# A fused convolution, attention and expert kernel: info and mask spread by DMA, not by products with ones

## The reference

```python
x = x + conv(group_norm(x))          # below
t = tokens(x)                        # 32*1024 tokens of 64 channels
t = t + attention(layer_norm(t))     # linear attention with elu+1, 8 heads, a layer norm inside, a 128-wide MLP, a layer norm
t = t + experts(layer_norm(t))       # top 2 of 8 experts, each 64 -> 128 (gelu) -> 64, summed with their weights
...
def conv(x):
    info = relu(info_w @ x + info_b)         # 16 channels
    mask = sigmoid(mask_w @ x + mask_b)      # 16 channels
    expanded = mask[:, None] * info[None]    # all 16*16 = 256 products per pixel
    return relu(out_w @ expanded + out_b)    # back to 64 channels
```

## Time and profile before

| what | us |
|---|---|
| median of 2 runs | 1132.91 (1130.81 to 1135.02) |
| profiled execution | 1131.8 |
| its span, first to last instruction | 1129.9 |
| PE, DVE, ACT, POOL busy | 1038.0, 735.4, 641.0, 404.9 |
| mean granted TensorE clock | 0.985 of full |

### The profile page before, as it was taken

One profiled execution on the slowest core, in us unless ns is written; L12 is line 12 of the kernel. 1 busy time (PEld: TensorE's weight loads), 2 busy tenths in 40 slices (PEclk: granted clock), 3 DMA queues, 4 the chain that ended last, 5 costly groups with the idle time before them and its releaser, 6 DMA issues. The chain is left out here.

```text
span 1129.9 us, 17149 instructions
## 1 busy us (share of the span) xinstructions
PE 1038.0 (92%) x6678; PEld 445.2 (39%) x6678; DVE 735.4 (65%) x1529; ACT 641.0 (57%) x867; POOL 404.9 (36%) x534
## 2 busy tenths in 40 slices
PE   4888699989999899989999899998999989998997
PEld 2453353324533245323543245332454334532232
DVE  5764744786648866587655966488655886646334
ACT  3354356665665655665656556655566655565554
POOL 0010031352323532344323533235333344224576
PEclk9997889999999999999999999999999999999999
DMA  5000095017700464006710078002760057200860
GB/s 162 6 1 1 1 204 136 21 31 166 164 1 20 97 157 106 1 20 149 160 51 1 19 154 205 1 20 54 157 148 1 19 107 167 50 1 19 198 142 19
DMA packets 15600, 88.66 MB, mean 78 GB/s; under 512 B 3488, under 2 KB 6816, under 8 KB 11424
## 3 DMA queue, kind: packets, MB, share of 16 engines
q1 hardware_dynamic: 15520, 87.57, 33.3%
HBM read 78.12 MB, written 9.44 MB: 77 GB/s over the span
## 5 line engine op out<-in xcount | busy, mean ns | idle before, releaser
L1048 POOL TENSOR_TENSOR XB<-TM,XB 128x256 f32<-128x256 f32 x508 | 366.1, 748 | 570.3 <-DVE TM L1360 570.1
L995 ACT ACTIVATE H<-HP,W 128x1024 f32<-128x1024 f32 x224 | 241.4, 1113 | 182.0 <-PE HP L849 181.7
L1360 DVE SCALAR_TENSOR_TENSOR TM<-HP,B2S,CWB 128x512 f32<-128x512 f32 x224 | 164.9, 747 | 163.7 <-PE HP L863 159.2
L849 PE MATMUL HP<-XF,W1E 64*128 64x512 f32 x1024 | 260.8, 620 | 4.4 <-DVE TM L1360 3.7
L863 PE MATMUL HP<-H,W 128*64 128x512 f32 x896 | 234.3, 613 | 24.2 <-ACT H L995 24.2
L849 PEld LDWEIGHTS HP<-XF,W1E 64*128 64x128 f32 x1024 | 86.2, 186 | 129.5 <-issue 59.7
L863 PEld LDWEIGHTS HP<-H,W 128*64 128x64 f32 x896 | 47.7, 135 | 164.9 <-ACT H L995 111.1
L933 ACT ACTIVATE T<-R 128x512 f32<-128x512 f32 x96 | 57.3, 598 | 45.4 <-PE R L642 38.4
L1161 DVE SCALAR_TENSOR_TENSOR BIG<-R,T 128x512 f32<-128x512 f32 x112 | 70.1, 683 | 14.0 <-PE R L606 13.9
L1248 DVE SCALAR_TENSOR_TENSOR BIG<-T,R 128x512 f32<-128x512 f32 x64 | 41.9, 685 | 38.0 <-ACT T L961 38.0
L606 PE MATMUL R<-IM,REP 32*128 32x512 f32 x336 | 51.3, 470 | 7.7 <-DVE RT L1348 4.4
(11 more groups left out here) (182 smaller groups left out, 1398.8 us busy)
## 6 DMA issues: line engine op xcount, KB each, us to landing
CWB<-gates_hbm SPq DMA_DIRECT2D x32, 1536.0 KB, 20.3
CWB<-gates_hbm SPq DMA_DIRECT2D x32, 512.0 KB, 6.6
out<-XB SPq DMA_DIRECT2D x15, 512.0 KB, 3.1
X<-x SPq DMA_DIRECT2D x14, 512.0 KB, 13.5
XF<-x SPq DMA_DIRECT2D x2, 512.0 KB, 5.9
gates_hbm<-RT SPq DMA_DIRECT2D x16, 64.0 KB, 1.6
W<-wpack SPq DMA_DIRECT2D x1, 968.0 KB, 4.7
W1E<-w1e SPq DMA_DIRECT2D x1, 512.0 KB, 7.2
```

The costliest lines, as they stand in the source:

```text
L849: last = mm(HP[u % BATCH][:, half(k)], W1E[img(k), e, :], XF[img(k), 1 - par, s, half(c)], start=True, stop=True)
L995: f(activated(b, u).rearrange("p k t -> p (k t)"), HP[u % BATCH][:, :], ACT.Gelu, bias=col(B1E + e))\
L1048: last = nc.gpsimd.tensor_tensor(acc, TM[:, u % BATCH, quarter(0, h)], acc, ALU.add)
L1360: v.scalar_tensor_tensor(out=TM[:, u % BATCH, :], in0=sums_of(b, u), scalar=B2S[:, e % 2, e // 2:e // 2 + 1], in1=CWB[:, s, e, half(c)], o ...
```

## The change

REP, IM, the 48 matmuls with ones, the 8 ACT copies and the DVE split are taken out. In their place SP issues DMAs as soon as ACT has written a slot's info and mask (im_act). For each slot: two writes of info to HBM (32 partitions, 64 KB each); four mask transfers for image 0, each from 8 partitions of T1 to 128 partitions of BIG, every row copied 16 times (256 KB each, pieces of 2 KB); one info load from HBM to all 128 partitions (512 KB, 16 rows copied 8 times); four mask transfers and one info load for image 1, which goes to XN. DVE then multiplies in place in BIG, 8 products of 1024 columns per group, all operands in SBUF. conv_out waits for all four products of its slot. SP's `prepare` DMAs now stand behind group 0's spreading. SCHEDULE and OPENING are dealt out anew.

```diff
@@ SP (gate_weights, last_weights, store unchanged) @@
+                def replicate(s):
+                    sp.wait_ge(im_act, nth(a + 1, s))
+                    for c in range(NCH):
+                        sp.dma_start(info_hbm[s][:, half(c)], T1a[strip(0, s, c), s, 0:CH]).then_inc(info_out[s], 16)
+                    masks(s, 0)
+                    sp.wait_ge(info_out[s], (a + 1) * 16 * NCH)
+                    info(s, 0)
+                    masks(s, 1)
+                    info(s, 1)
+                def info(s, k):
+                    sp.dma_start(INFO[k][:, s, :], info_hbm[s, IC * k:IC * k + IC, :].unsqueeze(0).broadcast_to([P // IC, IC, T]))\
+                        .then_inc(info_in[k][s], 16)
+                def masks(s, k):
+                    if k == 0 and s == G - 1 and a > EARLY:
+                        sp.wait_ge(lgt_ps, a)
+                    for h in range(2):
+                        for c in range(NCH):
+                            row = strip(1, s, c).start + IC * k + HD * h
+                            sp.dma_start(BIGa[:, s, 2 * k + h, half(c)],
+                                         T1a[row:row + HD, s, 0:CH].unsqueeze(1).broadcast_to([HD, P // HD, CH]))\
+                                .then_inc(mask_in[k][h][s], 16)
+                INFO = (T2a, XNa)
@@ PE @@
-                def replicate(n, slots):
...
-                        for part in range(2):
-                            for c in range(NCH):
-                                rows = strip(1 if n % 3 else 0, s, c)
-                                last = mm(Ra[s][:, half(c)], REP[rows, n, :], IM[rows, s, part, :], start=(part == 0), stop=(part == 1))
                 def conv_out(slots):
...
+                    if exists(a - 1) and a != EARLY:
+                        pe.wait_ge(cwt_done, a)
                     for s, c in pieces(slots):
-                        pe.wait_ge(prod_done[s], at(a * 4 + 4, c))
+                        pe.wait_ge(prod_done[s], a * 4 + 4)
@@ ACT @@
-                def info(k, slots):
-                    for s, c in pieces(slots):
-                        act.wait_ge(rep_ps[s], at(a * NREP + 3 * k + 1, c))
-                        f(T2a[:, s, half(c)], Ra[s][:, half(c)], ACT.Copy).then_inc(ir_done[s], 1)
@@ DVE @@
-                def info_mask(s):
-                    v.tensor_copy(high, T1a[:, s, 0:CH]).then_inc(hl_high, 1)
-                    v.tensor_tensor(IM[:, s, 1, :], T1a[:, s, 0:CH], high.bitcast(F32), ALU.subtract).then_inc(hl_done, 1)
                 def product(k, h, slots):
-                    for s, c in pieces(slots):
-                        if h == 0:
-                            dve.wait_ge(ir_done[s], at(a * 2 + k + 1, c))
-                        dve.wait_ge(rep_ps[s], at(a * NREP + 3 * k + h + 2, c))
-                        v.scalar_tensor_tensor(out=BIGa[:, s, 2 * k + h, half(c)], in0=Ra[s][:, half(c)], scalar=1.0,
-                                               in1=T2a[:, s, half(c)], op0=ALU.add, op1=ALU.mult)\
+                    for s in slots:
+                        dve.wait_ge(info_in[k][s], (a + 1) * 16)
+                        dve.wait_ge(mask_in[k][h][s], (a + 1) * 16 * NCH)
+                        v.scalar_tensor_tensor(out=BIGa[:, s, 2 * k + h, :], in0=BIGa[:, s, 2 * k + h, :], scalar=1.0,
+                                               in1=(T2a, XNa)[k][:, s, :], op0=ALU.add, op1=ALU.mult)\
                             .then_inc(prod_done[s], 1)
@@ SCHEDULE, one of its lines @@
-    ("info_0.1", "YY", 1, 2), ("low_0.0", "", 0, 0), ("low_0.1", "HH", 0, 0), ("high_0.0", "", 0, 0),
+    ("choose_2", "Y", 0, 2), ("info_mask_1", "HYHYHH", 0, 0), ("gate_rows", "Y", 2, 6), ("low_0.1", "YH", 3, 0),
```

More of the change, by code:

```diff
@@ L89 @@
 OPENING = [
[11 rows of a table removed]
-    "norm_4.0", "next conv_out.0", "next centre_1.1", "next centre_1.0", "gates", "next rstd_1", "gate_tokens",
-    "gate_exp", "choose_1", "choose_2", "gate_rows", "weights_1", "next norm_1.1", "next norm_1.0",
-    "next features_1.0", "next features_1.1",
+    "channel_stats", "group_stats", "group_norm", "next channel_stats", "info_mask_0", "info_mask_1", "low_0.0",
[9 rows of a table added]
+    "next centre_1.0", "next centre_1.1", "next rstd_1", "gates", "gate_tokens", "gate_exp", "choose_1", "choose_2",
+    "gate_rows", "next norm_1.0", "next norm_1.1", "next features_1.0", "weights_1", "next features_1.1",
 ]
@@ L254, in build @@
         im_act = sem("im_act")
-        hl_high = sem("hl_high")
-        hl_done = sem("hl_done")
-        rep_ps = sems("rep_ps")
-        ir_done = sems("ir_done")
+        info_out = sems("info_out")
+        info_in = [sems(f"info_in{k}_") for k in range(2)]
+        mask_in = [[sems(f"mask_in{k}{h}_") for h in range(2)] for k in range(2)]
         prod_done = sems("prod_done")
@@ L455, in _ @@
             sp.dma_start(W[:, 0:NW_FIRST], wpack[:, 0:NW_FIRST]).then_inc(w_in, 16)
-            def by_image(t):
-                return t.rearrange("p (k n c) -> p k n c", k=2, c=P)
-            rep = by_image(reps[:, 0:NREP * P])
             im_bias = wpack[:, COLS["cols"][0] + B_IM:COLS["cols"][0] + B_IM + 2]
-            for q in range(4):
-                there = slice(32 * q, 32 * q + 32)
-                sp.dma_start(by_image(raw_reps)[there, :, 0, :], rep[0:32, :, 0, :]).then_inc(r_in, 16)
-                sp.dma_start(by_image(raw_reps)[there, :, 1:3, :], rep[32:64, :, 1:3, :]).then_inc(r_in, 16)
             for q in range(4):
@@ L588, in info_mask @@
                     last.then_inc(im_ps, 1)
-                def replicate(n, slots):
-                    if n == 0 and starting(a):
-                        pe.wait_ge(act_prep, 2)
-                    for s in slots:
-                        if n == 0:
-                            pe.wait_ge(hl_done, nth(a + 1, s))
-                            if exists(a - 1) and a != EARLY:
-                                pe.wait_ge(cwt_done, a)
-                        elif n % 3 == 1:
-                            pe.wait_ge(ir_done[s], at(a * 2 + n // 3 + 1, LAST))
-                        else:
-                            pe.wait_ge(prod_done[s], at(a * 4 + (n + 1) // 3 + n // 3, LAST))
-                        for part in range(2):
-                            for c in range(NCH):
-                                rows = strip(1 if n % 3 else 0, s, c)
-                                last = mm(Ra[s][:, half(c)], REP[rows, n, :], IM[rows, s, part, :], start=(part == 0), stop=(part == 1))
-                                if part == 1:
-                                    last.then_inc(rep_ps[s], 1)
                 def conv_out(slots):
@@ L898, in _ @@
             act.wait_ge(w_in, 16)
[L899 to L900 removed]
             act.wait_ge(bi_in, 128)
             f(BT[:, :], BI[:, 1, 0:1], ACT.Copy, scale=0.5).then_inc(act_prep, 1)
[L903 removed]
+            act.wait_ge(act_prep, 1)
             f(ONE[:, 0:1], BI[:, 0, 0:1], ACT.Copy, bias=1.0, scale=0.0)
@@ L1003, in parts @@
                     "info_mask_0": lambda: info_mask(0), "info_mask_1": lambda: info_mask(1),
-                    **slotwise("info_0", lambda slots: info(0, slots)), **slotwise("info_1", lambda slots: info(1, slots)),
                     **slotwise("conv_out", conv_out), **slotwise("centre_1", lambda slots: square(1, slots)),
```

35 lines of the change are left out of this document (12 added, 23 removed), and 50 rows, old and new, of tables (OPENING, SCHEDULE).

## The result

The changed kernel takes **1566.96 us** (1564.34 to 1569.59, 2 runs), against 1132.91 before: ratio 1.383, 95% interval 1.378 to 1.388. It is slower by 38%. The forecast was 1670 in a range of 1150 to 1800. The profiled execution took 1564.34 us, its span is 1562.5 us, the mean granted clock 0.873.

What follows compares the result with a forecast made beforehand. PE, busy 92% of the span, was taken as the bound before, with DMA setting the interval up to conv_out afterwards. 1131.8 + 408 (six turns) + 131 (opening) = 1671, so 1670 us, range 1150 to 1800.

Steps and rivals of the forecast that it cites:

- Price of a mask transfer: Each 256 KB mask transfer from 8 partitions takes 5.2 us (50 GB/s), between 0.7 and 6.2 us.
- the rate follows the number of partitions touched: DMA rate goes by partitions touched on the SBUF side, not bytes: 381 GB/s for 128, 197 for 64.
- A group in 97 us: A group's DMA work, 16 x 5.2 + 4 x 2.7 + 1.2 = 95 us, lands its last piece at about 97 us.
- A turn +68 us: Each of six turns gets 68 us longer: conv_out at 100 us behind im_act in place of 30.6, 69.4 - 5 + 3.5.
- my -5 for work done early: In each turn, one first and four second expert layers more are done within the interval before conv_out: 5 us less.
- +3.5 for the clock: In each turn PE stands still some 60 us, so afterwards runs partly at 1.2 GHz: 10 x 0.35 = 3.5 us.
- The opening +131 us: The opening, without expert work to fill waits, gets 88 + 46 - 3 = 131 us longer.
- What hides: Router's weights queued behind the masks stay hidden, by a few microseconds; expert units keep their durations; PE slices show six deep gaps.
- Half speed: Rival: a mask transfer takes 2.6 us, a turn is 24 longer, the opening 48: 1324 us (1250 to 1450); chance 0.18.
- Like the router's weights: Rival: a mask transfer takes 1.3 us, a turn +2.5, the opening +23: 1170 us (1145 to 1195); chance 0.15.
- Full speed: Rival: masks at 381 GB/s, 0.7 us each, a group's 18 us hidden under expert layers: 1093 us (1075 to 1115); chance 0.21.
- PE's saving of 7.5 us counts in full: 6 x -7.5: In the full-speed rival, removing 48 matmuls with ones and their waits shortens each of six turns by 7.5 us.

Runs made afterwards that it cites:

- e1_step4: Changed kernel, with each mask transfer's 8 source rows on every 4th partition in place of 8 neighbours; 1285.49 us, ratio 1.134.
- e5_roles: Changed kernel with roles exchanged: mask spread once per image (16 rows on every 2nd partition, 8 copies), info loaded twice per image from HBM; 1188.25 us, ratio 1.050.
- e2_rows128: Changed kernel, but each mask transfer reads all 128 partitions of T1 once (mask wrong, sizes and counts kept); 1195.65 us, ratio 1.055.
- e6_all_fast: Changed kernel, but masks and infos both read all 128 partitions of T1 once, nothing through HBM (mask and info wrong); 1165.17 us, ratio 1.031.
- e7_rows16: Changed kernel, but each mask transfer reads 16 neighbouring rows 8 times in place of 8 rows 16 times (mask wrong); 1312.78 us, ratio 1.160.
- e12_all_fast_old: e6_all_fast with SCHEDULE and OPENING of the kernel before (mask and info wrong); 1148.24 us, ratio 1.013.

## Why the prediction was right

The direction and the chain of waits held, and the sizes were 17 to 26% too large. The rule by which the price was chosen was wrong in its form, and that the price itself came out right is in part luck.

- **Price of a mask transfer**, taken as 5.2 us between 0.7 and 6.2. Transfers by themselves move 50 GB/s, which is 5.2 us. I had it from "the rate follows the number of partitions touched". e1_step4 refutes this as it stands: also 8 partitions, and 136 GB/s; e5_roles reads 16 partitions at 195, as fast as the router's weights go to 64. What counts is how they lie. The rule worked here because the 8 rows are neighbours, as the rows that it was read from were. And the rows bounded the price only by 41 and 197 GB/s; that it was 50 to the digit is luck.
- **A group in 97 us** failed in size: the last landing comes 427.19 - 344.53 = 82.7 us behind im_act. The info load was taken too cheap, 2.7 us where one alone takes 4.0 (131 GB/s in e2_rows128), which makes the sum 100. The error that outweighs it is that I had added the transfers one by one. They run one by one only as long as they are alone. The four first do so (10.40 us for their issues, 50 GB/s); from the first info load on transfers overlap, 134 GB/s at 365, 87 in the gap. Which of them overlap with which is left open.
- **A turn +68 us**, measured +53.8. All of the error is the term before: 85.2 - 30.6 = 54.6, and my -5 for work done early and +3.5 for the clock make it 53.1. The clock term is near: with the same number of matmuls PE is busy 1026.2 us after and 1003.8 in e6_all_fast, 22.4 us or 3.2 for each of seven waits.
- **The opening +131 us**, measured +110.0. conv_out of slot 1 comes at 114.88 in place of 41.29, +73.6 for +88, again the group's time. For group 1 DVE waited 14.29, 23.48 and 4.30 us; I had 14 and 32. The masks start at 29.30 (29.6).
- **What hides** held: expert units keep their length at full clock, conv_out and not the router's weights ends the wait, the slices show the six gaps.
- **The rivals' times.** Half speed: 1324 forecast for 2.6 us a transfer, e7_rows16 has 2.7 and 1312.78. Like the router's weights: 1170 (up to 1195) for 1.3 us; no run has this price with all else as in the kernel after. e2_rows128, with 0.7, already needs 1195.65, so 1170 was too low. Its sum has info loads at 2.7 us and no wait for the info writes, against 4.0 and 8.5 us in e2_rows128; whether they are all of it is open. **Full speed: 1093 (1075 to 1115), e6_all_fast 1165.17: wrong.** The step that failed is "PE's saving of 7.5 us counts in full: 6 x -7.5", with the sentence that the removed matmuls can't have been hidden as "PE is full in their stretch". PE was full there, but DVE was busy for 25.8 of the same 30.6 us: with the matmuls gone, e12_all_fast_old reaches conv_out after 29.4 to 31.3 us in place of 30.6, PE being idle 19.3 us more in the turns. The products in SBUF, for which I had put "at most 0.2 us" each, took up to 0.53 more (1.75 against 1.22 us). In e6_all_fast itself the new lists come on top, 26 us in the turns. The 0.21 that I gave to faster stood on this step. Of all that was tried, no version that spreads by DMA was faster than before.

## What to carry to other kernels

A row copied from SBUF to many partitions by DMA is priced by where the source rows lie: neighbours are slow together, so put them four partitions apart (here 5.2 us became 1.9 for 256 KB) before counting bytes. An engine that is 92% busy is not proof that each operation taken from it counts in full: look whether another engine is nearly as busy in the same stretch, for then the work taken out comes back as a wait. Leaving half of the operation out is a cheap trial, but read from the trace how much busy time it really took away (here a third less for half of the matmuls), and don't double the result. If work moves from PSUM to SBUF operands on DVE, look at what POOL does beside it.

## What the runs showed of the hardware

- An issue on SP isn't short when the transfers ahead are slow: `L517` takes 0.597 us at least, 3.082 at the median and 4.752 at most in the kernel after, 0.614 at the median in e1_step4. SP issues from 344.6 to 418 without rest, and what stands behind (gates_hbm) goes late.
- The DMA share reads 0.46 while transfers are at the bound of their source partitions, 0.91 for 16 neighbours at 98 GB/s, and 1.02 for 128 rows at 385 GB/s. The share doesn't say how far the rate is from the best.
- With no work on PE the granted clock can read 1.00 or 0.50 for the same stretch: 34 to 38 us of the opening had 1.00 in the kernel after and 0.50 in e7_rows16 and e1_step4.
- An info load (16 rows of HBM, each copied 8 times) alone moves 131 GB/s at a share of 0.53.
